# A hand-ordered transformer block on one core: the first steps of the tile after the next move to the end of each round, and the output projection is handed over by pairs

## The reference

```
p    = hidden @ cond_in_W                    # 128 wide, read as 64 pairs
new  = rotate(state, theta) + p_t            # scan over time: a rotating state
cond = rmsnorm(states) * w;  deltas = cond @ delta_W
ctrl = hidden @ ctrl_W + b                   # q, k, v, decay, beta, gate
q,k,v = silu(causal_conv4(q_l + qd)) ...     # per channel
S_t  = g_t S_{t-1} + k_t b_t (v_t - k_t g_t S_{t-1})    # delta rule, 16 heads of 16
o    = rmsnorm(q_t S_t) * silu(gate);  x += o @ out_proj_W.T + b
x   += differential_attention(layernorm(x), ctx of 64 tokens), 32 half heads of 8
x   += ffn(layernorm(x)):  h = x + silu(pw(conv3(x)));  8 experts, top 2, weighted
       rmsnorm, gelu feed-forward of 64
```

## Time and profile before

| | |
|---|---|
| median of 3 runs | 1618.92 us |
| the profiled execution | 1627.61 us |
| its span | 1625.8 us, mean granted clock 0.979 |
| PE busy | 1519.0 us, 93% |
| DVE busy | 1179.9 us, 73% |
| ACT busy | 830.7 us, 51% |
| POOL busy | 209.2 us, 13% |
| `x1` of tile 0 done | 220.4 us |
| `x1` of tiles 1 to 7 done | 405.0, 589.8, 771.1, 954.3, 1138.9, 1323.7, 1489.6 us |

### The profile page before, as it was taken

How to read it: one execution, slowest core, us unless ns; L and a number is a source line. 1 busy time by engine, 2 the same in 40 slices (tenths; PEclk the granted TensorE clock), 3 DMA queues, 4 the chain that set the end, 5 groups by cost and what they waited for, 6 DMA issues and landing times.

```text
span 1625.8 us, 39269 instructions
## 1 busy us (share of the span) xinstructions
PE 1519.0 (93%) x16376; PEld 1024.8 (63%) x16376; DVE 1179.9 (73%) x3193; ACT 830.7 (51%) x1594; POOL 209.2 (13%) x212
## 2 busy tenths in 40 slices
...
DMA packets 20215, 31.32 MB, mean 19 GB/s; under 512 B 1480, under 2 KB 17864, under 8 KB 19784
## 3 DMA queue, kind: packets, MB, share of 16 engines
...
## 4 chain that ended last, share of the span: by engine, by line
PE 72%; DVE 22%; ACT 3%; issue 3%; POOL 0%; DVEq 0%; ACTq 0%
PE bank L1808 14%; PE bank L1756 6%; PE bank L1530 5%; PE bank L1416 5%; PE bank L1746 4%; PE bank L1459 4%; PE bank L1732 4%; PE four L1615 4%; PE bank L1441 3%; PE bank L1531 2%; PE four L1634 2%; PE bank L1523 2%; PE four L1683 2%; DVE qkv L1038 2%; PE bank L1422 2%
## 5 line engine op out<-in xcount | busy, mean ns | idle before, releaser
L1808 PE MATMUL bank<-w_sb,cs 128*128 128x512 f32 x512 | 246.9, 602 | 0.0
L521 POOL TENSOR_TENSOR decayed<-state,pk 128x512 f32<-128x512 f32 x64 | 74.4, 1163 | 925.5 <-DVE state L1167 925.5
L797 ACT ACTIVATE cs<-bank 128x512 f32<-128x512 f32 x128 | 76.2, 596 | 172.0 <-PE bank L1422 149.1
L1808 PEld LDWEIGHTS bank<-w_sb,cs 128*128 128x128 f32 x512 | 95.1, 191 | 90.9 <-issue 80.1
L1459 PEld LDWEIGHTS bank<-c_sb 128*128 128x128 f32 x1056 | 134.2, 200 | 24.8 <-issue 17.8
L1364 DVE SCALAR_TENSOR_TENSOR cs<-cs,rwt 128x256 f32<-128x256 f32 x224 | 98.7, 482 | 70.2 <-ACT cs L797 70.1
L1459 PE MATMUL bank<-c_sb 128*128 128x128 f32 x1056 | 140.3, 286 | 5.0 <-DMA c_sb<-in_consts 5.0
L1756 PE MATMUL bank<-vx_sb,cs 128*128 128x136 f32 x1024 | 134.0, 283 | 6.3 <-ACT cs L751 6.3
L1756 PEld LDWEIGHTS bank<-vx_sb,cs 128*128 128x128 f32 x1024 | 125.2, 190 | 22.7 <-ACT cs L751 14.5
L751 ACT COPY cs<-bank 128x512 f32<-128x512 f32 x128 | 74.7, 584 | 116.7 <-PE bank L1746 115.8
L1530 PE MATMUL bank<-hT,w_sb 128*128 128x512 f32 (+1 forms) x224 | 109.7, 613 | 6.2 <-ACT pre L598 4.0
...
## 6 DMA issues: line engine op xcount, KB each, us to landing
...
```

Of the source, the lines that this page charges most:

```text
L1808: mm(dst, x1T[:, k, b * TB:b * TB + TB], ew[:, k, ep * 512:ep * 512 + 512], start=k == 0, stop=False)
```

## The change

- A third set of steps is in each round, marked "*": steps of `first(i + 2)`. They are `ln1`, `turn1`, `rot` (the two projections and products) and `gate.0`. The scan that was the end of `rot` is a DVE step of its own, `scan`, and stays in the round of the next tile. There is one round more, i = -2, in which tile 0 has its "*" steps; no fillers are issued in it.
- `sum.0`, `sum.1` and their `sq` and `rs` now close the round before ("+"). `sq` writes the tile `osq`, and no longer waits for `lt_ps`, `beta` and `proj_ps`.
- `spread` is now at the end of the round before. Its output `xpand` lies in a part of `pre`; it waits for the last `conv` and for `mkq` of the tile before instead of `x1`. `decay` itself waits for both `x1`.
- The output projection goes by pairs: `og.0`, `og.1`, `wo.1`, `wo.2`, `x1.0`, `x1.1`, each with its own event. `ln2` of a pair waits for that pair's `x1`.
- The tile of the gates, `sgs`, has five parts in a ring instead of two of two.
- `bv` on POOL stands between `dec.4` and `dec.5` instead of after both `ffd`.
- Both tables are new in all places. The fillers that are issued become 396: 66 in round -1, 133 in round 0, 13 in each of the rounds 1 to 6, 59 in round 7 and 60 in round 8. (The entries of `KEEP` for round -2 issue nothing.)

```diff
 ORDER = {
     "pe": steps('''
-        cs.7.1 co.7.0 co.7.1 -ffu.0 -ffd.1 onorm.0 onorm.1 wo.0 -ffu.1 wo.1'''),
+        -mo.1 co.6.0 d1.7 co.6.1 *turn1.0 cs.7.0 -ffd.0 cs.7.1 co.7.0 co.7.1 -turn6.1 -ffu.0 -ffd.1 *turn1.1 onorm.0
+        onorm.1 *rot.0 -ffu.1 wo.0 *rot.1 wo.1 *gate.0 wo.2 +sum.0 +sum.1'''),
...
-            for i in range(-1, NI + 1):
-                if i + 1 < NI:
-                    firsts[i + 1] = firsts.get(i + 1) or first(i + 1)
-                halves = {1: firsts.get(i + 1), 0: firsts.pop(i, None), -1: prologue if i == 0 else second(i - 1) if i > 0 else None}
+            for i in range(-2, NI + 1):
+                if i + 2 < NI:
+                    firsts[i + 2] = firsts.get(i + 2) or first(i + 2)
+                halves = {2: firsts.get(i + 2), 1: firsts.get(i + 1), 0: firsts.pop(i, None), -1: prologue if i == 0 else second(i - 1) if i > 0 else None}
...
                     up("lgc")
+                    up("halo", 4)
                     if i:
-                        pool.wait_ge(ev["x1"].sem, ev["x1"].at(i - 1))
+                        pool.wait_ge(ev["mkq"].sem, ev["mkq"].at(i - 1, 8))
...
-                    if j == 0:
-                        up("lt_ps")
-                        up("beta", 2)
-                        up("proj_ps", 6)
+                    if j == 0 and i:
+                        act.wait_ge(ev["osum"].sem, ev["osum"].at(i - 1, 2))
                     up("silu", j + 1)
...
-                    fin("sq", A((rota, rotb)[j % 2][:, :], qkv[:, j, :], ACT.Square))
+                    fin("sq", A(osq[:, j % 2, :], qkv[:, j, :], ACT.Square))
...
                     fin("rot_sb", tt(r3(rotb[:, :]), r3(bank[7][:, :]), sinb, ALU.mult))
+
+                def scan():
+
                     up("rot_sb", 2)
...
+                def og(k):
+
+                    if k == 0:
+                        ch.wait()
+                    for g in range(G):
+                        at = slice(D * k, D * k + D)
+                        last = tt(kn[:, g, at].rearrange("p (b c t) -> p b c t", b=2, c=NC), oT.rearrange("p (c k g b t) -> p k g b c t", c=NC, k=2, g=G, b=2)[:, k, g, :, :, :],
+                                  sgs[:, (2 * i + g) % 5, at].rearrange("p (b c t) -> p b c t", b=2, c=NC), ALU.mult)
+                    fin("og", last)
+
+                def x1_(n):
+                    up("wo_ps", n + 1)
...
                     if i:
-                        pe.wait_ge(ev["x1"].sem, ev["x1"].at(i - 1))
+                        pe.wait_ge(ev["x1"].sem, ev["x1"].at(i - 1, 2))
                     mm(bank[2][:, :], C("tri"), xpand, start=True, stop=True)
...
-                    up("og")
-                    for p in range(2):
-                        last = pair_to_tokens(p, bank[2 + p][:, :], kn, wo)
-                    fin("wo_ps", last)
+                    p = k - 1
+                    up("og", k)
+                    fin("wo_ps", pair_to_tokens(p, bank[2 + p][:, :], kn, wo))
```

More of the change, by code:

```diff
@@ L116 @@
     "pe": steps('''
-        sum.0 sum.1 decay -turn2.0 sum.2 grow -turn2.1 -qx.0 sum.3 -sc.0.0 -qx.1 -sc.0.1 vturn raw.0 raw.1 -sc.1.0
-        -sc.1.1 -pt.0 raw.2 raw.3 -pt.1 raw.4 raw.5 -pv.0 -sc.2.0 -sc.2.1 +turn1.0 -pt.2 raw.6 -pt.3 raw.7 +turn1.1
-        -pv.1 +rot.0 -sc.3.0 -sc.3.1 -pt.4 d1.0 -pt.5 -pv.2 -sc.4.0 -sc.4.1 -pt.6 -pt.7 +rot.1 -pv.3 -sc.5.0 -sc.5.1
-        +gate.0 -pt.8 -pt.9 +unrot -pv.4 +gate.1 -sc.6.0 -sc.6.1 -pt.10 +cond -pt.11 z.0 -pv.5 -sc.7.0 -sc.7.1 z.1
-        cs.0.0 +db -pt.12 cs.0.1 z.2 -pt.13 +proj.0 -pv.6 z.3 d1.1 -turn3.0 +btr -pt.14 co.0.0 +brep.0 co.0.1 cs.1.0
```

151 lines of the change are left out of this document (71 added, 80 removed), and 6 rows, old and new, of the table KEEP.

## The result

The changed kernel takes 1639.8 us (median of 4 runs, 1639.4 to 1640.2) against 1618.2 (1615.5 to 1622.0): 1.0132 times as long, 95% interval 1.0111 to 1.0153. The forecast was 1610, faster, with 1595 to 1627 as its range; it was wrong in sign. The profiled execution took 1639.9 us (span 1638.1) against the 1627.6 on which the sum was made, so between the profiles the kernel lost 12.3 us where a gain of 9.0 was forecast.

What follows compares the result with a forecast made beforehand. Taken as bounds: PE from `z` to round end, DVE from `raw` to `z`, a chain at the round's end. Five rounds -15.0, rounds 6, 7 and the rest -8.0, start +14.0: -9.0 us, 1618.9 to 1610; range 1595 to 1627.

Steps and rivals of the forecast that it cites:

- The rest: Last `second`, behind tile 7's `x1`: only fillers change, 40 fewer, 6 of them on the path; -1.3 us, bounds -4 and +3.
- The clock: Rival, chance 0.10: mid-round, PE short of work gets one more half-rate stretch in each of 8 rounds; +14 us, 1624.
- three signs of being wrong: `sum.0` of tile 0 before 97, a middle round not shorter, or PE's half-rate stretches changing by more than four.
- The middle: `raw` to first `z`, rounds 1 to 5: DVE and PE each lose 6.3 us of work; -6.2 us a round.
- that bound of 3.5: `raw` to `z`: smallest gain, 3.5 us a round, if as much turns into waits for the softmax's own chain.
- The scan stays: `raw` to `z` on DVE: `scan` is not among the work that leaves this stretch; no size given.
- The start: Tile 1's moved steps stand on tile 0's path: `raw` +13.0 us (bounds 8 and 15), +14.0 up to tile 0's `x1`.
- The end of round 0: Tile 2's `ln1` adds +2.6 us to the chain of chunks, and the longer end +1.8.
- The other steps of a round: Rounds 1 to 5: last `co` to `x1` +1.8 us, `x1` to `decay` -0.4, `decay` to `raw` +0.9, `z` to last `co` +0.9.
- the rounds gain nothing: Rival, chance 0.17: `gate.0` between `wo.1` and `wo.2` delays a chain that doesn't catch up; 0 a round, 1628.
- The table loads: Second pair among the experts: one silu 1.8 us late, costing nothing; rival, chance 0.02: 4.6 late, PE stops some 2 us, 1624.
- From profile to median: Median 8.7 us below the profiled run before; same difference after the change: 1618.9 - 9.0 = 1610 us.

## Why the prediction was wrong

The measured median is 29.9 us above the forecast: 21.3 us between the forecast change and that of the profiles, and 8.6 in the step from profile to median.

**The rest** made 12.0 of the 21.3 us. The step: "In the last `second` only fillers change; I take -1.3", with +3 as its worst end. I had priced fillers as rows of 0.112 us, that is as work that might stand on the path, and not by what they do where PE would idle. The clock was a rival in the text, but looked for in the middle of the rounds; in the rest, where round 8 lost 54 of its 114 fillers (the forecast said 40; 32 by the rows of the stretch) and the softmax alternates between three engines without any other work to put between, it wasn't asked. Taking 56 away from the kernel before costs 11.7 us; giving them back to the changed kernel, without the 25 that collide with round 7's, returns 7.9. The text named three signs of being wrong, and none showed: `sum.0` came at 107.3, the middle rounds got shorter, and there were 15 stretches at half clock instead of 16. Counted by number the clock had not changed; by time it went from 69.1 to 89.7 us.

**The middle** made 2.7 us in each round at full clock and 10.0 in rounds 1 to 5, as much as the whole 9.6 by which these missed. The step: "Since DVE sets this stretch, its loss counts." DVE sets its dense part; in the head, up to the transposes, PE is busy throughout and DVE waits, and 5.2 of DVE's 6.5 us stood there (statistics, normalisation and `turn1`'s copy; the terms of the forecast add up to 6.5, not 6.3). That the bound of 3.5, "if as much turns into waits for the softmax's own chain", is the number that came is luck: removal alone gave 1.5 (46.0 to 44.5), less than that bound, and the new order the other 2.0, 0.7 in the head and 1.3 in the dense part, out of which `scan` and `unrot.0` had moved. "The scan stays" gave this move no price, though the part on the start names the scan's new place.

**The start** had the right mechanism, and its sum (+14.8 against +14.0) by luck, from two errors that cancel. `raw` came 4.8 us later than forecast and beyond its bound: the last `conv` ended at 89.6 instead of 86.9, mostly by the first round's own new fillers and step order (with tile 1's steps taken back it still ended at 89.1), and the chain behind it took 17.7 us instead of 16.1 to 16.5. The end of round 0 came out 4.5 us better (+0.3 and -0.4 where +2.6 and +1.8 were counted): 24 fillers had stood there before, whose place the new steps took. I had counted neither. Taking the steps back, with the old fillers and order, returned 16.3 us in the profiles.

**The other steps of a round** came near their numbers (-0.6, +0.7, +1.0, +1.5 for -0.4, +0.9, +0.9, +1.8). The +1.0 of `z` to `co` is partly luck: the normalisation was to last 1.3 to 2.7 us and lasted 3.38, with PE's wait of 1.7 us for it. The rival "the rounds gain nothing" is the one that came nearest: rounds 1 to 5 gained 1.1 us each, under the 1.5 below which it was to decide, and `gate.0` between the projections does cost what it lasts, 1.7 us a round. But this cost was in the sum already (+1.8); what was missing was the middle's gain.

**The table loads** cost nothing among the last experts, as said. Three experts earlier they stopped PE for 2.55 us, about the rival's price, but by their place and not by the longer hold that the rival took: they lasted 1.28 us each there too.

**From profile to median** I shifted both by the same 8.7 us. The profiled run of before was one with a low mean clock: in 17 later runs of it the time goes from 1613.8 us at a mean granted clock of 0.989 to 1627.3 at 0.980. The changed kernel's 4 runs lie within 0.8 us of each other and of its profile. Of the 21.7 us between the medians 9.4 come from this. The step that failed here is "the same difference on it gives": the new kernel's profile lies 0.1 us above its median, not 8.7.
